# Retention stage of a 12-sublayer kernel: the start offsets of four interleaved tiles, 0, 2, 5, 7 steps against 0, 0, 5, 5

## What is computed

```python
def group_norm(y, g, b):                     # per head, 8 heads of 32
    yh = (yh - mean(yh)) * rsqrt(var(yh) + EPS)
    return yh.reshape(y.shape) * g + b
def msr(x, ...):
    q, k, v = x @ Wq, x @ Wk, x @ Wv
    scores = einsum('bnhd,bmhd->bhnm', q, k) * D      # D: causal decay per head
    y = einsum('bhnm,bmhd->bnhd', scores, v)
    return jax.nn.silu(x @ Wg) * group_norm(y, gg, gb) @ Wo
for i in range(2):
    ret = msr(layer_norm(x), ...) + x
    x = gelu(layer_norm(ret) @ W1[i] + b1[i]) @ W2[i] + b2[i] + ret
```

## Time and profile before

| | us |
|---|---|
| median of 3 runs | 4538.15 (4524.79 to 4539.03) |
| profiled execution | 4520.55, its span 4518.7 |
| TensorE matmul busy | 3612.0 (80%) |
| VectorE busy | 2635.7 (58%) |
| ScalarE busy | 1766.7 (39%) |
| GpSimd busy | 358.6 (8%) |
| retention stage, in the span | 3738.77 to 4138.79 |

### The profile page before, as it was taken

One profiled execution on the slowest core, in us unless ns is written; L12 is line 12 of the kernel. 1 busy time (PEld: TensorE's weight loads), 2 busy tenths in 40 slices (PEclk: granted clock), 3 DMA queues, 4 the chain that ended last, 5 costly groups with the idle time before them and its releaser, 6 DMA issues. The chain is left out here.

```text
span 4518.7 us, 69708 instructions
## 1 busy us (share of the span) xinstructions
PE 3612.0 (80%) x26668; PEld 2573.3 (57%) x26672; DVE 2635.7 (58%) x5422; ACT 1766.7 (39%) x3341; POOL 358.6 (8%) x566
## 2 busy tenths in 40 slices
PE   7999999987768887826888669788888876885777
PEld 5555657876755564613565535455555555664666
DVE  6889884442567878765444462367767653443443
ACT  4888881112353443412323112244444422322333
POOL 3000000000000000000111000011111101110000
PEclk8556559998876666657988789899999988988788
DMA  2000001000010000010000121000000002000000
GB/s 76 1 0 0 0 0 70 0 8 11 12 49 1 0 0 0 0 57 5 7 3 7 57 56 74 2 3 3 3 3 5 3 1 113 1 1 1 1 1 10
DMA packets 43830, 72.80 MB, mean 16 GB/s; under 512 B 25693, under 2 KB 33377, under 8 KB 40293
## 3 DMA queue, kind: packets, MB, share of 16 engines
q1 hardware_dynamic: 35432, 70.54, 4.4%
q10 hardware_dynamic: 8256, 0.52, 0.2%
HBM read 67.91 MB, written 3.15 MB: 16 GB/s over the span
## 5 line engine op out<-in xcount | busy, mean ns | idle before, releaser
L1316 DVE TENSOR_SCALAR_CACHE_REDUCE l0x_ex<-l0x_s_ps 128x1024 f32<-128x1024 f32 x258 | 305.6, 1222 | 56.5 <-PE l0x_s_ps L1019 55.6
L1151 ACT ACTIVATE l0x_ex<-l0x_ex,l0x_neg_max,l0x_q_scale 128x2048 f32<-128x2048 f32 x128 | 268.0, 2094 | 51.8 <-DVE l0x_neg_max L1322 50.0
L1019 PE MATMUL l0x_s_ps<-l0x_kT,l0x_qT 64*128 64x512 bf16 x516 | 231.8, 591 | 34.0 <-ACT l0x_qT L1146 19.9
L1031 PEld LDWEIGHTS l0x_t_ps<-l0x_identb,l0x_pb 128*128 128x128 bf16 x2048 | 196.8, 141 | 109.0 <-issue 53.2
L1158 ACT ACTIVATE l0x_pt<-l0x_t_ps 128x1024 bf16<-128x1024 bf16 x256 | 246.1, 1013 | 26.2 <-PE l0x_t_ps L1031 25.9
L1031 PE MATMUL l0x_t_ps<-l0x_identb,l0x_pb 128*128 128x128 bf16 x2048 | 230.5, 301 | 7.7 <-ACT l0x_pt L1158 4.0
L1331 DVE TENSOR_SCALAR l0x_pb<-l0x_ex 128x2048 bf16<-128x2048 f32 x128 | 156.3, 1222 | 0.0
L263 PE MATMUL l3x_bank<-l3x_wproj,l3x_cat 128*128 128x256 f32 x512 | 121.3, 391 | 32.2 <-DVE l3x_cat L3345 32.2
L263 PE MATMUL l3x_bank<-l3x_w_kv_x,l3x_ctxT 128*128 128x512 f32 x256 | 130.5, 658 | 0.9 <-ACT l3x_ctx_q L762 0.9
L263 PEld LDWEIGHTS l3x_bank<-l3x_wproj,l3x_cat 128*128 128x128 f32 x512 | 96.5, 193 | 52.6 <-DVE l3x_cat L3345 38.7
L840 ACT ACTIVATE l3x_e<-l3x_e 128x1024 f32<-128x1024 f32 x24 | 25.4, 1057 | 250.4 <-DVE l3x_e L860 250.4
(11 more groups left out here) (741 smaller groups left out, 8697.7 us busy)
## 6 DMA issues: line engine op xcount, KB each, us to landing
l3x_wproj<-in_L_xattn_wproj SPq DMA_DIRECT2D x1, 4096.0 KB, 25.4
l3a_w<-in_L_attn_W SPq DMA_DIRECT2D x2, 2048.0 KB, 12.6
l2f_w<-in_L_ffn_w SPq DMA_DIRECT2D x1, 2816.0 KB, 11.6
l0x_ctxT<-in_ctxT SPq DMA_DIRECT2D x8, 256.0 KB, 2.9
l0a_wq<-in_L_attn_W_Q SPq DMA_DIRECT2D x1, 2048.0 KB
l0a_wk<-in_L_attn_W_K SPq DMA_DIRECT2D x1, 2048.0 KB
l0a_wv<-in_L_attn_W_V SPq DMA_DIRECT2D x1, 2048.0 KB, 7.9
l0a_wo<-in_L_attn_W_O SPq DMA_DIRECT2D x1, 2048.0 KB, 13.3
```

What stands on the lines that cost most here:

```text
L1019: ins = mm(s_ps[:, j * 512:(j + 1) * 512], qT[rows, h // 2, :], kT[rows, h // 2, j * 512:(j + 1) * 512], start=True, stop=True)
L1031: ins = nc.tensor.transpose(t_ps[:, j * P:(j + 1) * P], pb[:, h % 2, j * P:(j + 1) * P], identb[:])
L1151: s.activation(ex[:, h % 4, :], ex[:, h % 4, :], ACT.Exp, scale=q_scale[:, h:h + 1], bias=nb[:, h:h + 1], accum_out=sums[:, h:h + 1]).then ...
L1316: v.tensor_scalar(ex[:, h % 4, c], s_ps[:, c], 1.0, None, ALU.mult, ALU.max, accum_out=mx[:, h, half:half + 1]).then_inc(o.up(scores_taken ...
```

## The change

Way n begins `5 * (n // 2)` steps late in place of `n * 5 // 2`: 0, 0, 5, 5 in place of 0, 2, 5, 7. The same line serves all four compute engines. No instruction, buffer or semaphore differs, only the order in which the ways' segments stand in each stream.

```diff
         def in_its_turn(n, program, eng):
-            yield from steps(n * 5 // 2)
+            yield from steps(5 * (n // 2))
             for t in range(TILES // WAYS):
                 yield from program(eng, t)
```

## The result

The changed kernel takes 4493.07 us as the median of 4 runs (4490.81 to 4500.9), the kernel before in the same series 4535.27. The ratio, which is taken over all the runs, is 0.9914 with a 95% interval of 0.9892 to 0.9935: 39 us less, between 29 and 49 (the two medians lie 42 us apart). A second series gave 0.9927 (0.9913 to 0.994), 33 us less. The forecast was 28 us less, at 4510, with a range of 4486 to 4532. The sign and the range hold; the gain came out larger than forecast. The second series lies inside the band of 19 to 34 us that had most of the chance, the first above it.

A forecast was written before the change was run, and what follows sets the result against it. TensorE's work plus holes waiting on VectorE and GpSimd chains was taken to bound the stage: 337.3 walked plus 34.7 clock gives 372.0 us, 28.0 less than 400.0. Kernel 4510 us, range 4486 to 4532.

The forecast's parts named there:

- large holes: Stage, steps 0 to 2, 5 to 8, 20 to 22: TensorE waits for VectorE's in-order chain, 14.9 us each.
- Hole c: Stage, step 11, transposes of the inner norm and of group-normed y: VectorE's chain makes it 7.35 us.
- Hole d: Stage, step 13: second decay product, two normalisations, then the transposes, 2.8 us.
- Hole e: Stage, steps 16 and 17 up to the q, k, v matmuls: VectorE's chain makes it 6.1 us.
- Sum 337.3: Whole stage walked at full clock, dense stretches plus holes: head 142.2, 20-step period 166.3, tail 28.8 us.
- In the steady part the change moves idle time together, it does not remove any.: Repeating 20 steps of the stage: 166.3 us after against 131.4 work plus 34.8 idle, 166.2, before.
- The ends: Stage's head and tail, where one tile began and ended alone: always two tiles afterwards, 13 us gained.
- The clock term: Stage time lost to half clock: 49.6 us before, 34.7 after, with fewer slow stretches, about 11 against 17.
- One: Stage: holes as worked out but clock still costs 45 to 49.6 us, stage 382 to 387; chance 0.16.
- two: Whole kernel: no change, 4530 to 4545 us, old idle at the ends hidden another way; chance 0.10.
- Three: Behind large holes the clock stays low; three whole slow blocks give stage about 444, kernel 4582 us; chance 0.06.
- Four: Stage: clock costs 25 us or less and hidden gaps close too, stage 360 to 364; chance 0.10.

The follow-up runs named there:

- changed_no_beta: Changed kernel without the addition of gn_beta in the y chain, run once for its trace: stage 365.0 us, a large hole 14.6 us.
- changed_filled: Changed kernel with extra TensorE matmuls of constants, never read, before the waits in its holes: stage 339.7 us, kernel 0.9865 of before.
- the filled kernels: Kernel before and changed kernel, each with unread matmuls of constants before TensorE's waits: stages 364.6 and 339.7 us, medians 4499.6 and 4476.3.

## Why the prediction was right, and where it was not

**The holes and the dense blocks.** Right. 14.9 for the large holes: 14.84 filled, 15.35 to 15.56 unfilled. Hole c 7.35: 7.4 filled, 7.6 unfilled. Hole d 2.8: 2.6. Hole e 6.1: 6.1. No wait for gelu or decay stands inside a block, and VectorE's chains set the length of the large holes (changed_no_beta). Sum 337.3: 339.7 filled, and 2.0 of the 2.4 are in the tail (30.8 where 28.8 had been taken). That the two O run at half clock in a hole is hidden, and so is nearly all other slow work there: it also is why TensorE's idle time is 59.6 us and not the 74.6 of the walk, as slow matmuls fill part of the holes.

**"In the steady part the change moves idle time together, it does not remove any."** This step failed. I set 166.3, a walk at full clock, against 131.4 + 34.8 from the trace, but the 34.8 are the idle time of an order that ran partly at half clock. Slow matmuls run while a chain runs that TensorE would wait for at full clock, so idle plus full-clock work is too low. Like with like is way 0's first add to its second in the filled kernels, first the one before, then the changed one:

```profile
3890.17 0.43 DVE L3922 TENSOR_TENSOR x_stream<-x_stream,l3a_cur 128x256 f32<-128x256 f32 x1
4061.26 0.42 DVE L3922 TENSOR_TENSOR x_stream<-x_stream,l3a_cur 128x256 f32<-128x256 f32 x1
```

```profile
3887.28 0.42 DVE L3922 TENSOR_TENSOR x_stream<-x_stream,l3a_cur 128x256 f32<-128x256 f32 x1
4053.89 0.42 DVE L3922 TENSOR_TENSOR x_stream<-x_stream,l3a_cur 128x256 f32<-128x256 f32 x1
```

That is 171.1 us before and 166.6 after, 4.5 less. The 166.3 was right for the new order, the 166.2 for the old one was not.

**The ends.** I gave them the whole structural gain, 13 us. At full clock it is 24.9, of which the tail behind way 0 has 15.1 (54.3 against 39.2 in the filled kernels) and the head up to its first add 5.3. So the ends have 20.4 us: the place was mostly right, the size too small; a walk of the old order in the same manner would have given the 29 us at once (366.7 - 338.0), with no subtraction of measured idle.

**The clock term.** 34.7 was forecast for the changed order, 31.0 and 23.9 measured, against 49.6 for the old order, where 35.4 is measured. The 49.6 held slow work that was hidden and the pipeline ends; counted in the same way the changed stage has 370.7 - 262.7 - 59.6 = 48.4, so "49.6 goes to 34.7" was 15 us of gain that did not exist as such; it stood in for the structure that the two steps above lost (13 where 24.9 was there), and the two errors nearly cancel in 372.0. That this number came so near to 370.7 is luck. Inside the term the sizes were off, as the table of changed_filled has them: a large hole costs 1.2 to 2.1 us (for the first, P, P from 3785.27 takes 1.5 more than at full clock, and the hole 0.5) where I had 4.2, and hole d costs 6.6 or nothing where I had 0.8. "Fewer holes, so less clock" holds for the path only (35.4 to 31.0 or 23.9): the granted clock fell to 0.84, and more of the half clock now lies where it does little harm.

**The rivals.** One (the clock costs what it does now) did not come, two neither. Three, that the clock stays low through a block behind a large hole, is refuted for the holes of 15 us: full clock was back at most 4.4 us after the start of the first P, in both profiles. (Its 444 us for three slow blocks does not follow from its terms, 372.0 + 3 x (29.5 - 4.2) = 447.9, and a hole of 14.9 us is longer than any other in the stage, not in the whole trace.) It is true in kind for hole d, which I had put at 0.8. Four, a clock that costs 25 us or less and a stage of 360 to 364, had a chance of 0.10, and the second profile is just that (23.9 and 363.6), though not by gaps that closed: by one hole d without a fall. For the fall itself the prediction had named the Trainium skill, TensorE: Matmul & The Clock Gate, "Why this matters for your kernels": idle gaps between bursts let the clock fall. The traces agree that it falls behind such gaps. The price here did not go by the length of the gap, but by how much work on the path ran slow behind it: the hole with 1.70 us of idle cost 6.6, the holes of 15 us 1.2 to 2.1.

**From stage to kernel.** The two profiles show 29.3 and 36.5 us in the stage; the two series 39 (29 to 49) and 33 (27 to 39). These agree within what they can tell. For the order before there is a single profile of the stage, so whether its 400.0 is typical to better than some 7 us stays open.

## What to carry to other kernels

For streams with a fixed order, list which segments stand beside each other in each step, cost dense stretches from start to start and holes by the sum of the other engine's in-order work, and do it in full for both orders: never set a walk at full clock against idle time measured at half clock. Align tiles so that a short segment with a long chain behind it stands beside a long one, look at the ends for how many tiles still run there, and try the distance between pairs (three steps were 16 us better than five at full clock, 17 to 24 as they run). Where a short idle stands right ahead of a long block of matmuls, a few matmuls of constants in it can be worth a good part of what the order is: 9 to 16 us of the stage here, for four of them in each of two holes, where the change of the order brought 29 to 37.

## What the runs showed of the hardware that I had not expected

- A wait of 1.70 us, with 0.89 us of transposes behind it, was followed by 13.65 us at half clock in three of the four such holes of the two profiles of the changed kernel (G, G, H, H took 19.0 us and not 12.3), and by full clock in the fourth. With the hole filled it did not happen in either tile. In the kernel before, twelve of sixteen waits of about that length were followed by full clock.
- Matmuls whose result nobody reads kept the granted clock at 0.98 to 0.99 through the stage. In the changed kernel they delayed no dense block, and three of the four filled stages are within 2.1 us of the walk (339.7 against 338.0 for the changed one).
- The same code ahead of the stage took 3735.1 to 3759.0 us up to it in these profiles, a spread as large as the gain looked for.
